# Fused SSM and MoE layer on one core: GpSimd forms two tiles of u per instruction, and its DMA work moves between the pairs

## What is computed

```
dt = softplus(xn @ dt_w.T + dt_b);  A = -exp(log_A)
b = xn @ B_w.T + B_b;  c = xn @ C_w.T + C_b
h[d,n] = exp(A[d,n]*dt[d]) * h[d,n] + (dt[d]*xn[d]) * b[n]     # step by step over the sequence
y[d]   = sum_n h[d,n]*c[n] + D_skip[d]*xn[d]
```

## Time and profile before

| what | us |
| --- | --- |
| median of 3 runs | 4012.66 |
| profiled execution | 4012.38 |
| its span on the core | 4010.7 |
| DVE busy | 3699.5 (92%) |
| PE busy | 3328.8 (83%) |
| POOL busy | 3252.5 (81%) |
| ACT busy | 2529.3 (63%) |

### The profile page before, as it was taken

How to read it: one execution, slowest core, us unless ns; L and a number is a source line. 1 busy time by engine, 2 the same in 40 slices (tenths; PEclk the granted TensorE clock), 3 DMA queues, 4 the chain that set the end, 5 groups by cost and what they waited for, 6 DMA issues and landing times.

```text
span 4010.7 us, 70861 instructions
## 1 busy us (share of the span) xinstructions
PE 3328.8 (83%) x16548; PEld 2166.8 (54%) x16548; DVE 3699.5 (92%) x2500; ACT 2529.3 (63%) x4779; POOL 3252.5 (81%) x1722
## 2 busy tenths in 40 slices
PE   7697788888887888888887888878887888888887
PEld 4375555555555555555555555555555555555554
DVE  6797999989999999999998999989999999999997
ACT  3213666766666667666666667667666667666665
POOL 0004989888888989888898999889888999888886
PEclk9898999999999999999999999999999999999998
DMA  9954666565666656575666656575667656575666
GB/s 326 342 75 117 158 152 154 137 164 150 161 151 171 156 147 146 138 177 151 157 159 167 159 146 148 138 173 157 160 154 172 156 142 148 138 178 149 158 160 155
DMA packets 382792, 646.23 MB, mean 161 GB/s; under 512 B 86717, under 2 KB 258881, under 8 KB 382081
## 3 DMA queue, kind: packets, MB, share of 16 engines
q1 hardware_dynamic: 289458, 539.05, 48.6%
q0 software_dynamic: 67776, 85.24, 13.8%
q10 hardware_dynamic: 25104, 16.91, 1.9%
HBM read 515.68 MB, written 142.80 MB: 164 GB/s over the span
## 4 chain that ended last, share of the span: by engine, by line
issue 27%; POOL 26%; PE 12%; SPq 11%; DVE 8%; DMA 7%; ACT 6%; POOLq 1%; ACTq 1%; DVEq 0%
POOL u L1003 16%; SPq L331 7%; PE bank L627 5%; POOL out_rows L962 5%; DMA dt<-dt_rows 3%; DVE h L1194 3%; PE bank L574 3%; POOL xg L950 3%; DVE hc L1183 3%; SPq L319 3%; ACT bank L775 2%; DMA dt<-x 2%; DMA w_sb<-w 2%; ACT ht L817 1%; PE bank L534 1%
## 5 line engine op out<-in xcount | busy, mean ns | idle before, releaser
L1003 POOL TENSOR_TENSOR u<-dtx,b_sb 128x1024 f32<-128x1024 f32 x1024 | 2492.4, 2494 | 232.9 <-DVE h L1194 203.8
L1194 DVE TENSOR_TENSOR_SCAN h<-bank,u 128x1024 f32<-128x1024 f32 x1024 | 2302.3, 2277 | 44.0 <-ACT bank L775 30.6
L775 ACT ACTIVATE bank<-dt,a_neg 128x1024 f32<-128x1024 f32 x1026 | 1129.0, 1108 | 548.7 <-DMA dt<-dt_rows 247.3
L627 PE MATMUL bank<-xgt,w_sb 128*128 128x256 f32 x4096 | 1088.2, 412 | 349.9 <-ACT ht L817 163.6
L1183 DVE TENSOR_TENSOR hc<-h,bank 128x2048 f32<-128x2048 f32 x514 | 1165.0, 2267 | 175.8 <-ACT bank L845 175.2
L627 PEld LDWEIGHTS bank<-xgt,w_sb 128*128 128x128 f32 x4096 | 782.1, 201 | 746.4 <-issue 650.7
L636 PE MATMUL bank<-w_sb,ht 128*128 128x256 f32 x4096 | 938.8, 382 | 49.5 <-ACT o_sb L832 32.3
L636 PEld LDWEIGHTS bank<-w_sb,ht 128*128 128x128 f32 x4096 | 762.4, 190 | 244.6 <-issue 149.2
L817 ACT ACTIVATE ht<-bank,b_sb 128x256 f32<-128x256 f32 x1024 | 424.0, 464 | 313.6 <-PE bank L627 279.4
L586 PE MATMUL bank<-hc,rsum 128*32 128x512 f32 x4112 | 552.7, 610 | 4.2 <-DVE hc L1183 4.2
L962 POOL DMA_INDIRECT out_rows<-o_sb,sidx x258 | 415.6, 1611 | 124.8 <-issue 65.0
(11 more groups left out here) (105 smaller groups left out, 1866.9 us busy)
## 6 DMA issues: line engine op xcount, KB each, us to landing
b_sb<-bc_rows SPq DMA_DIRECT2D x1032, 128.0 KB
c_sb<-bc_rows SPq DMA_DIRECT2D x1032, 128.0 KB
dt<-dt_rows SPq DMA_DIRECT2D x528, 128.0 KB, 4.4
dtx<-dtx_rows SPq DMA_DIRECT2D x528, 128.0 KB, 2.8
w_sb<-w SPq DMA_DIRECT2D x18, 1024.0 KB, 9.8
dt_rows<-dt_n SPq DMA_DIRECT2D x137, 128.0 KB, 3.1
dtx_rows<-dtx_n SPq DMA_DIRECT2D x137, 128.0 KB
out_rows<-y_sb POOLq DMA_DIRECT2D x34, 512.0 KB
```

What stands on the lines that cost most here:

```text
L627: mm = pe.matmul(m_ps[:, c, :], w1_sb[:, kk, ch * P:(ch + 1) * P], xgt[:, kk, :], start=(kk == 0), stop=(kk == KD - 1))
L775: act.activation(a_ps[k % 2], dt[:, k % GPP, :], ACT.Exp, scale=a_neg[:, col:col + 1]).then_inc(a_ready, 1)
L1003: pool.tensor_tensor(u[:, k % UB, :], dtx[:, gp, :], b_sb[:, j, :], ALU.mult).then_inc(u_ready, 1)
L1194: dve.tensor_tensor_scan(h[:, k, :], a_ps[k % 2], u[:, k % UB, :], 0.0, ALU.mult, ALU.add).then_inc(scan_done, 1)
```

## The change

POOL's loop over k goes in steps of two. One instruction writes u of tiles k and k+1 (2048 columns): the two dtx tiles lie beside each other, and B is read twice by a broadcast. It waits for the scan of tile k+1-4 in place of k-4, and u_ready rises by 2 at its end. What POOL does besides is laid anew: both gathers behind the first pair (before: one behind tile 0, one behind tile 1); add_y and dtx_part behind the second pair (before: add_y behind tile 0, dtx_part behind tile 5); the scatters behind the third and the fourth pair (before: behind tiles 4 and 6).

```
-                    for k in range(NG):
+                    for k in range(0, NG, 2):
...
                         if ng == 0 and k < GPP:
-                            pool.wait_ge(dtx_in[gp], 16 * R * (hf + 1))
-                        pool.wait_ge(scan_done, st * NG + k - UB + 1 + SCAN0)
-                        pool.tensor_tensor(u[:, k % UB, :], dtx[:, gp, :], b_sb[:, j, :], ALU.mult).then_inc(u_ready, 1)
-                        if k == 0 and adds:
-                            pool.wait_ge(y_evac, 2 * hf + ng + 1)
-                            pool.wait_ge(o_scattered, 16 * SJ * (st + 1))
-                            settle(pool)
-                            add_y((hf + 2 * B - 2 + ng - 1) % (2 * B), ng - 1)
-                        if k < SJ:
-                            gather(st + 1, (s + 1) % 2, k)
-                        if k == 5:
+                            for i in range(2):
+                                pool.wait_ge(dtx_in[gp + i], 16 * R * (hf + 1))
+                        pool.wait_ge(scan_done, st * NG + k + 1 - UB + 1 + SCAN0)
+                        pool.tensor_tensor(u[:, k % UB:k % UB + 2, :], dtx[:, gp:gp + 2, :],
+                                           b_sb[:, j, :].unsqueeze(1).to_broadcast([P, 2, S]), ALU.mult).then_inc(u_ready, 2)
+                        if k == 0:
+                            for i in range(SJ):
+                                gather(st + 1, (s + 1) % 2, i)
+                        if k == 2:
+                            if adds:
+                                pool.wait_ge(y_evac, 2 * hf + ng + 1)
+                                pool.wait_ge(o_scattered, 16 * SJ * (st + 1))
+                                settle(pool)
+                                add_y((hf + 2 * B - 2 + ng - 1) % (2 * B), ng - 1)
                             dtx_part(NG + 1 + st, (b + 1 + (s + 1) // NG) % 2, (s + 1) % NG)
                         if k in (4, 6):
                             scatter(st, (s + 1) % 2, k // 2 - 2, 2 * b + ng if adds else None)
```

## The result

The changed kernel took 4179.53 us (median of 4 runs, 4174.39 to 4190.49), the kernel before, run beside it, 4013.15 (4011.36 to 4016.86): ratio 1.0417, 95% interval 1.0395 to 1.0439. It is slower, as forecast, and inside the range of 4070 to 4185, but 58.5 us beyond the forecast of 4121. The profiled execution took 4174.39 us with a span of 4172.5, 161.8 more than before.

The account below looks back on a forecast made before the run. The prediction took DVE to bound the kernel, with losses where halves change; 55 + 31 + 4 + 0.5 + 5 + 7 + 6 = 108.5 us on 4012.4 gave 4121 us, range 4070 to 4185.

Parts of the forecast that it names:

- Ordinary steps: Steps away from a change of half: claimed to stay at 26.57 us, all in time by 1.5 to 2.1 us.
- rival (d): POOL's pair takes over 4.95 us by the repeated read of B and every step grows: about 4600 us, chance 0.04.
- SP's list: SP's in-order loads in the last step: dtx(0) waits for the pair, so dtx(1) goes out 4.56 us later.
- Rival (c): SP's loads have slack: transfers set dt(1)'s landing, which could stay; 4012 to 4000, say 4008 us, chance 0.06.
- I expect every change of half to look like that one: 8.0, less 0.3: At each change of half DVE waits as in the trace's first change: 7.7 us against 5.3 before.
- second wait: DVE's later wait for c_copy in the new step, 1.43 us in the pattern; forecast to be absent.
- POOL's lag: POOL still 0.45 us late in the last step after the second add_y step: 16 times, 7 us.
- Rival (a): At changes of half PE's clock falls and the second wait stays: 4.6 us each, 4172 us, chance 0.16.
- 23 ordinary changes: Changes of half without a wait for weights, the first one apart: 2.4 us more each, 55 us.
- at most 7.5 us, so landed by 12.6, no delay: In add_y steps, add_y issued at 5.1 lands before the scatter at 12.5 needs it: no delay.
- rival (b): add_y's landing takes 10 us under load and holds the scatter: 44 us more, 4165 us, chance 0.12.

Follow-up runs that it names:

- Experiment 1: The changed kernel with each pair of u formed by two instructions of 1024 columns, wait and signal kept: 4193.93 us, ratio 1.0438.
- experiments 2 and 3: 2: kernel before, dtx(0) reload waiting for u of tile 6, ratio 1.0388; 3: changed kernel, last steps tile by tile, dtx_part behind tile 5, ratio 1.0145.
- experiment 5: The changed kernel with SP's two stores and c(1) issued ahead of dtx(0), and dt(0) ahead of dtx(2): 4110.46 us, ratio 1.0250.
- experiment 4: The changed kernel with add_y moved behind the first pair, ahead of the gathers: 4145.54 us, ratio 1.0327.

## Why the forecast came out on the right side and too small

1. *Ordinary steps.* They stay at 26.57 us, and the pair takes what was worked out. The view of line 1004 after (ns, min, median, max):

```profile
L1004 POOL TENSOR_TENSOR u<-dtx,b_sb x512: 4492/4547/5181, 358.2 to 4126.2; 128x2048 f32<-128x2048 f32 x171
```

4.547 us against 4.54: rival (d) is out, and so is any gain from the saving, which DVE covers. Experiment 1 adds that the long instruction has no part in the loss.

2. *SP's list.* Right in place and nearly in size: 7.0 us later for dtx(0), 5.4 for dt(1) in the step shown (4.9 in the mean of the mid-sequence changes) and 4.5 ahead of a next sequence, where POOL isn't late, against 4.56. Shown from both sides by experiments 2 and 3. But the reason may have been told by half. I counted SP's issues; b(0), which moves too, was not in my sum, and the DMA engines then have no work from 4 to 8 us of the step (experiment 5). How the loss divides between late issues and idle DMA engines is open. Rival (c) said that the transfers set the landing and that dt(1) could then stay where it was. It is out: dt(1) landed 5.0 us later in the mean of the mid-sequence changes (35.5 of the step, 30.5 before), as much as its issue moved.

3. *What a late dt(1) costs.* The step "I expect every change of half to look like that one: 8.0, less 0.3" held for the mid-sequence changes: two waits, 6.9 us in the step shown, and no second wait late in the new step. Their 3.4 each against 2.85 (2.4 and POOL's lag) is a matter of size, 10 us in all. It failed for the changes to the next sequence without weights. Timeline of DVE after, such a change:

```profile
2014.88 0.42 DVE L1108 SCALAR_TENSOR_TENSOR dt_n<-zv,bank 128x256 f32<-128x256 f32 x1 [2.78 <-ACT bank L760]
...
2022.71 2.29 DVE L1186 TENSOR_TENSOR hc<-h,bank 128x2048 f32<-128x2048 f32 x1 [4.98 <-ACT bank L845]
...
2028.17 2.29 DVE L1197 TENSOR_TENSOR_SCAN h<-bank,u 128x1024 f32<-128x1024 f32 x1 [0.98 <-ACT bank L775]
...
2038.17 2.29 DVE L1186 TENSOR_TENSOR hc<-h,bank 128x2048 f32<-128x2048 f32 x1 [1.15 <-ACT bank L845]
```

Four waits, 9.9 us, where I had put 7.7. The number was carried from one mid-sequence change over to all, in before (5.3; these cost 6.1 there) and in after. In means over these changes the two waits of the forecast are as in mid sequence (before prep_dt 2.7 against 3.1, before the first weigh 4.8 against 4.7), but the waits late in the new step, 2.5 us before, do not go away as they do there (2.8 after). That is 21 of the 50 us that the loop's forecast fell short.

4. *Rival (a)*, 4172, came nearest to the measured time, and by luck: it kept the second wait at all 23 ordinary changes, and the runs keep it only at those to the next sequence and put the rest at add_y. It blamed a fallen clock. The windows of the same change after:

```profile
2010.00:2014.00 4.00, 0.00 (x0) 0.00 (x0) 2.10 (x1) 1.12 (x2) 2.36 (x3) 0.94 1.02 240
2014.00:2018.00 4.00, 3.47 (x8) 2.86 (x9) 2.71 (x2) 0.67 (x2) 2.28 (x1) 0.50 1.05 227
2018.00:2022.00 4.00, 4.00 (x15) 2.57 (x17) 0.00 (x0) 1.05 (x1) 2.91 (x2) 0.71 1.06 239
2022.00:2026.00 4.00, 1.89 (x14) 1.09 (x7) 3.29 (x2) 1.07 (x4) 0.00 (x0) 1.00 1.03 247
```

PE rested from 2010 to 2014, ran at 0.50 (1.2 GHz) until about 2020 and was back at 1.00 (2.4 GHz) from 2022, before the wait at 2027. ACT's timeline shows what held the late decays, those of tiles 1 and 2:

```profile
2020.95 1.12 ACT L775 ACTIVATE bank<-dt,a_neg 128x1024 f32<-128x1024 f32 x1 [6.29 <-DMA dt<-dt_rows]
...
2026.95 1.12 ACT L775 ACTIVATE bank<-dt,a_neg 128x1024 f32<-128x1024 f32 x1 [3.88 <-issue]
```

The decay of tile 2 came 6.0 us behind that of tile 1; in mid sequence it comes 2.1 behind. It needs dt(2), but that load is not the reason: it was issued from 2015.9 to 2017.1 and took at most 5.9 us to land, so it was there at 2023.0, 3.9 us before. What lies at that place and not in mid sequence is the end of ACT's program loop over the sequences (line 800), which starts over between the two. At all 15 changes to a next sequence ACT sat idle for 2.9 to 5.4 us before this decay (2.0 to 5.6 in the kernel before), with dt(2) landed 3.0 to 5.2 us before it (1.1 to 5.7); at the 16 in mid sequence it was idle for at most 0.2 in either kernel. The wait of the scan of tile 2 (0.98) comes from this turn of ACT's loop; that the later wait (1.15) does too is likely and not shown. Both kernels have the turn, and the forecast, made from one mid-sequence change, could not see it. Why it takes so long, and what the kernel would gain without it, no run tests.

5. *add_y.* The step "at most 7.5 us, so landed by 12.6, no delay" failed. The 7.5 came from the kernel's end, with nothing else in flight; in the loop the median is 7.8. In the first of the two steps add_y went out at 5.0, as worked out, and the scatter did not wait. In the second it went out at 6.5, not 6.0, since POOL came late out of the first; there lie all 15 waits of the scatter, 29.3 us, and the second steps with add_y cost 28 us instead of 5: 23 of the missing 50. With the lag that they hand to the last step (experiment 4: 12 us; 7 were in the sum) it is rival (b) at half its price: moving add_y brought back 36 us by the ratios, of which 12 were forecast and 44 more were the rival's.

## What to carry to other kernels

When two instructions become one, ask first who else reads their signal. Here the next engine had buffers enough, but an in-order DMA queue released its loads on the same count, one tile of the pair came some 6.6 us later, and 4% of the time went (a fifth of it by add_y's new place), for 0.7 us a step saved on an engine with slack. Look at a burst as a whole, at when the DMA engines first have work and at the bytes that they have moved, and not only at the one load that is waited for: moving single loads up gave back far less than expected, since others then came late. These traces suggest, but no run isolates, that early idle time is not made good when the engines run at share 1.0 afterwards. And a price read from one instance holds for its kind only: a change to the next sequence, in the same trace, shows other waits. When a wait is longer at one kind of change, look at what the waiting engine did last before you blame the load: the landing time in the trace settles it.

## What the runs showed of the hardware

- A DMA of 512 KB that adds to DRAM, issued by GpSimd under load, took 5.8 to 8.3 us from issue to landing, median 7.8. By the Trainium skill (DMA: Bandwidth & Descriptors, section "Anatomy of one DMA — SWDGE") the estimate was 3.2; the runs do not agree.
- In a burst of loads the 16 DMA engines moved 225 to 262 GB/s at a share of 1.02 to 1.06; SP's issue of eight 128 KB loads took 3.60 us and in the denser burst of experiment 5 4.07 and 4.94 us.
- Where its program loop over the sequences starts over, ACT sat idle for 2.0 to 5.6 us before the next decay, and for the last 1.1 us of that or more the load that it needs had landed (15 turns in each of the two kernels).
